# A graph network on one core: the round loop written out, and the leaky ReLU made by ScalarE's Prelu

## The reference

```python
h = jnp.maximum(_layernorm(x, axis=-1), 0.0)
x = x + _L0_gnn_ref(h, adj, ...)      # attention, then two hops
h = jnp.maximum(_layernorm(x, axis=-1), 0.0)
x = x + _L1_gnn_ref(h, adj, ...)      # three graph convolutions
# in L0:
Xw = X @ Wv + bv
e = jax.nn.leaky_relu(sj[:, None, :] + si[:, :, None] + ab[0], negative_slope=0.2)
alpha_matrix = A * jnp.exp(e)
transition = alpha_matrix / (jnp.sum(alpha_matrix, axis=-1, keepdims=True) + 1e-12)
for k in range(3):
    H = H + Xk @ Wk[k] + bk[k]
    Xk = jnp.einsum('bij,bjd->bid', transition, Xk)
return jax.nn.relu(H)
```

## Time and profile before

| what | value |
|---|---|
| median of 3 runs | 897.61 us (896.24 to 898.79) |
| the profiled execution | 896.19 us |
| its span (first to last instruction) | 894.2 us |
| instructions in the trace | 22245 |
| TensorE matmul busy | 873.0 us |
| VectorE busy | 780.2 us |
| ScalarE busy | 629.5 us |
| GpSimd busy | 443.3 us |
| granted TensorE clock, mean | 0.994 of full speed |

### The profile page before, as it was taken

How to read it: one execution, slowest core, us unless ns; L and a number is a source line. 1 busy time by engine, 2 the same in 40 slices (tenths; PEclk the granted TensorE clock), 3 DMA queues, 4 the chain that set the end, 5 groups by cost and what they waited for, 6 DMA issues and landing times.

```text
span 894.2 us, 22245 instructions
## 1 busy us (share of the span) xinstructions
PE 873.0 (98%) x6480; PEld 818.2 (92%) x6480; DVE 780.2 (87%) x2065; ACT 629.5 (70%) x1543; POOL 443.3 (50%) x532
## 2 busy tenths in 40 slices
PE   8799999999999999999999999999999999999996
PEld 7699999899998999989999999998999999999996
DVE  5789999899898999989999899989999899999972
ACT  4477777677777777777777677776777677777773
POOL 4455454455454455455454455454555454555552
PEclk9899999999999999999999999999999999999999
DMA  8112122122121122121121121121121121221001
GB/s 195 41 32 56 35 60 59 32 59 54 34 59 48 41 59 55 34 59 46 43 59 50 39 59 46 43 59 41 48 59 45 44 59 41 48 59 47 26 26 35
DMA packets 107819, 45.44 MB, mean 51 GB/s; under 512 B 72560, under 2 KB 107504, under 8 KB 107760
## 3 DMA queue, kind: packets, MB, share of 16 engines
q1 hardware_dynamic: 106672, 43.81, 19.4%
q10 hardware_dynamic: 1088, 1.05, 0.4%
HBM read 28.05 MB, written 16.78 MB: 50 GB/s over the span
## 4 chain that ended last, share of the span: by engine, by line
PE 92%; issue 2%; DVE 1%; SPq 1%; POOL 1%; ACT 1%; DMA 1%; DVEq 0%; ACTq 0%; POOLq 0%
PE bank L873 41%; PE bank_p L873 35%; PE bank_turned L873 6%; PE bank_T L873 4%; PE bank_turned L884 3%; PE bank_T L894 2%; SPq L272 1%; DMA bias_col<-in_L_gnn_b 1%; ACT s_hi L517 0%; DVE h0T_lo L639 0%; POOL w_gcn_lo L372 0%; DVE p0b L716 0%; PE bank_p L1029 0%; POOL y__lo L345 0%; POOL bias_h L388 0%
## 5 line engine op out<-in xcount | busy, mean ns | idle before, releaser
L345 POOL TENSOR_TENSOR y__lo<-y_full,y__hi 128x256 fp32r<-128x256 f32 x256 | 191.5, 762 | 101.0 <-ACT y_full L534 101.0
L336 POOL TENSOR_TENSOR rstd<-veps,minus_half 128x2 f32<-128x2 f32 x128 | 95.5, 746 | 250.6 <-DVE veps L606 250.6
L873 PE MATMUL bank_p<-w_p_hi,h0T_hi 128*128 128x258 f32 (+1 forms) x512 | 176.4, 360 | 1.0 <-POOL w_p_lo L367 1.0
L873 PE MATMUL bank_p<-w_p_lo,h0T_hi 128*128 128x258 f32 (+1 forms) x512 | 165.3, 339 | 0.0
L873 PE MATMUL bank_p<-w_p_hi,h0T_lo 128*128 128x258 f32 (+1 forms) x512 | 142.7, 340 | 5.9 <-DVE h0T_lo L639 5.9
L873 PE MATMUL bank<-w_gcn_hi,y__hi 128*128 128x256 f32 x512 | 132.9, 292 | 1.5 <-ACT y__hi L534 1.3
L873 PE MATMUL bank<-w_gcn_lo,y__hi 128*128 128x256 f32 x512 | 127.9, 283 | 0.0
L534 ACT ACTIVATE y__hi<-bank,bias_col 128x256 fp32r<-128x256 f32 x256 | 119.8, 468 | 3.0 <-PE bank L873 3.0
L534 ACT ACTIVATE y_full<-bank,bias_col 128x256 f32<-128x256 f32 x256 | 121.7, 475 | 0.0
L361 POOL TENSOR_TENSOR adjT_lo<-adjT_full,adjT_hi 128x256 fp32r<-128x256 f32 x64 | 64.5, 1008 | 85.5 <-ACT adjT_hi L440 85.5
L873 PEld LDWEIGHTS bank_p<-w_p_hi,h0T_hi 128*128 128x128 f32 x512 | 97.3, 190 | 7.2 <-POOL w_p_lo L367 1.2
(11 more groups left out here) (94 smaller groups left out, 2346.7 us busy)
## 6 DMA issues: line engine op xcount, KB each, us to landing
x_in<-in_x SPq DMA_DIRECT2D x64, 256.0 KB, 2.9
x_new<-x_out SPq DMA_DIRECT2D x64, 256.0 KB, 2.2
adj_blocks<-in_adj SPq DMA_DIRECT2D x256, 32.0 KB, 2.1
w_raw<-in_L_gnn_Wk ACTq DMA_DIRECT2D x3, 256.0 KB, 6.9
w_raw<-in_L_gnn_W SPq DMA_DIRECT2D x3, 256.0 KB, 5.8
bk_bc<-in_L_gnn_bk SPq DMA_DIRECT2D x1, 384.0 KB, 6.2
wv_raw<-in_L_gnn_Wv ACTq DMA_DIRECT2D x1, 256.0 KB, 3.7
aw_bc<-in_L_gnn_aw SPq DMA_DIRECT2D x1, 256.0 KB, 5.4
```

The lines of the kernel that those rows point to most:

```text
L336: pool.tensor_tensor(rstd[n][k % 2][:], veps[n][k % 2][:], minus_half[:], ALU.pow)\
L345: pool.tensor_tensor(y[n][1][:, c], y_full[n][:, c], plain(y[n][0][:, c]), ALU.subtract)\
L873: return pe.matmul(dst, stationary, moving, start=start, stop=stop, skip_group_check=True)
```

## The change

The loop goes: `rounds(one)` calls `one(i, i % ROUND)` for i from 0 to 66, so each engine's program is straight-line code, with plain numbers in every wait. ScalarE's `logits` uses Prelu with alpha = 0.2 where it used Identity, so `z` holds the leaky ReLU at once. VectorE's instruction and the semaphore `leaky_made` go, and `exponentials` waits for `z_made`, which ScalarE itself raises.

```diff
-        def rounds(eng, one):
-
-
-            for i in range(ROUND):
-                one(i, i)
-            with eng.Fori(0, N_PAIRS // BODY - 1) as turn:
-                for k in range(BODY):
-                    one(turn * BODY + (ROUND + k), k % ROUND)
-            for i in range(N_PAIRS - ROUND, N_PAIRS + LAG_D):
+        def rounds(one):
+
+            for i in range(N_PAIRS + LAG_D):
                 one(i, i % ROUND)
...
         def after(i, n):
 
-            return not isinstance(i, int) or i >= n
+            return i >= n
...
-                act.activation(z[k % 2][:, 0, :], spread_ps[:, 0, :], ACT.Identity, bias=uv[k % 2][:, 0, 0:1])
-                act.activation(z[k % 2][:, 1, :], spread_ps[:, 1, :], ACT.Identity, bias=uv[k % 2][:, 1, 0:1])\
-                   .then_inc(z_made, 1)
+                for g in range(G):
+                    last = act.activation(z[k % 2][:, g, :], spread_ps[:, g, :], ACT.Prelu,
+                                          bias=uv[k % 2][:, g, 0:1], alpha=SLOPE)
+                last.then_inc(z_made, 1)
 
             def exponentials(i, k):
-                act.wait_ge(leaky_made, i + 1)
+                act.wait_ge(z_made, i + 1)
...
-            def leaky(i, k):
-                dve.wait_ge(z_made, i + 1)
-                zz = z[k % 2][:]
-                dve.scalar_tensor_tensor(zz, zz, SLOPE, zz, ALU.mult, ALU.max).then_inc(leaky_made, 1)
...
                 if a is not None:
-                    leaky(a, k)
                     turn_adj(a, k)
```

More of the change, by code:

```diff
@@ L40 @@
 ROUND = 4
-BODY = 2 * ROUND
 LAG_B, LAG_C, LAG_D = 1, 2, 3
@@ L193, in gnn_kernel @@
         z_made = sem("z_made")
-        leaky_made = sem("leaky_made")
         exp_made = sem("exp_made")
@@ L215, in gnn_kernel @@
         out_made = sem("out_made")
-        def rounds(eng, one):
-            for i in range(ROUND):
-                one(i, i)
-            with eng.Fori(0, N_PAIRS // BODY - 1) as turn:
-                for k in range(BODY):
-                    one(turn * BODY + (ROUND + k), k % ROUND)
-            for i in range(N_PAIRS - ROUND, N_PAIRS + LAG_D):
+        def rounds(one):
+            for i in range(N_PAIRS + LAG_D):
                 one(i, i % ROUND)
         def here(i, lag):
-            if isinstance(i, int) and not 0 <= i - lag < N_PAIRS:
-                return None
-            return i - lag
+            return i - lag if 0 <= i - lag < N_PAIRS else None
         def first(i):
-            return isinstance(i, int) and i == 0
+            return i == 0
         def second(i):
-            return isinstance(i, int) and i == 1
+            return i == 1
         def tail(i):
-            return isinstance(i, int) and i >= N_PAIRS
+            return i >= N_PAIRS
         def after(i, n):
-            return not isinstance(i, int) or i >= n
+            return i >= n
         def landed(i, k):
@@ L312, in one @@
                     store(n, (k - LAG_D) % ROUND)
-            rounds(sp, one)
+            rounds(one)
             for k in range(ROUND):
@@ L408, in one @@
                     gcn_weights_low()
-            rounds(pool, one)
+            rounds(one)
         @block.scalar
@@ L573, in one @@
                     adjT_high(a, k)
-            rounds(act, one)
+            rounds(one)
         @block.vector
@@ L800, in first_round @@
                 p2_low(0, 0)
-                leaky(0, 0)
                 moments(0, 1, 1, lambda: attention(0, 0))
@@ L861, in one @@
                     p0_bias(a, k)
-            rounds(dve, one)
+            rounds(one)
         @block.tensor
@@ L1072, in one @@
                     z1_product(b)
-            rounds(pe, one)
+            rounds(one)
 _OUT = "x_new"
```

## The result

The changed kernel takes 882.42 us (median of 4 runs, 881.72 to 883.34) against 897.22 us before (median of 4 runs). The ratio is 0.9834, with a 95% interval of 0.9817 to 0.9851: 1.7% faster, where 1.1% was forecast.

The account below looks back on a forecast made before the run. TensorE, busy 873.0 of 894.2 us, was taken as the bound. The 56 rounds -11.2, pauses +2.0, start and end -0.5 made -9.7 us, so 887.9 us on the median's scale; range 885.5 to 893.9.

Parts of the forecast that it names:

- the mechanisms of the back edges and of `rstd`: Loop branches stall VectorE's sequencer; GpSimd's `rstd` is held 0.12 us by the leaky ReLU's two SBUF operands.
- The wait at `aT_hi`: TensorE's weight load in each round: earlier `rstd` closes the wait, rounds of 13.23 us, 56 rounds -11.2 us with edges.
- The pauses: VectorE sequencer stops at code-block changes in straight-line code: about 7 in 56 rounds, +2.0 us.
- Start and end: Rounds 0 to 3 gain 0.2 us and rounds 60 to 63 gain 0.3 through the same chain: -0.5 us.
- The edges: Six loop back edges, VectorE waiting before `h0T_lo`, 1.2 us each: -7.1 us once written out.
- the 9.0 us lost: Loop's 56 rounds take 752.11 us against 743.1 at ordinary length; split into 1.9 for pauses and 7.1 for edges.
- Prelu in place of Identity: ScalarE's two activations from PSUM: same time as Identity's 368 and 360 ns; rival of slow Prelu, chance 0.02.
- VectorE's 0.42 us as such: Leaky ReLU's busy time in each of 64 rounds, mostly off TensorE's path: its removal by itself gains nothing.
- One table load: ScalarE: Prelu shares Exp's table; rival of separate tables, 2.57 us of loads a round, about 980 us, chance 0.05.
- The other bound of `rstd`: Rival on GpSimd: the transpose holds `rstd` at 0.81 us too, rounds of 13.31, 893.3 us, chance 0.26.
- The stream as the bound: Rival: instruction fetching of straight-line code stops engines; 909 us at two in three stops, up to 921, chance 0.05.
- No pause at all, 885.5: Low end of the forecast range: written-out code in which no block change falls on TensorE's path.

Follow-up runs that it names:

- the run with a short body: Kernel before with 4 rounds in the loop's body instead of 8, so 13 back edges instead of 6: 888.14 us, ratio 0.9902.
- the shifted loop: Loop kept, leaky ReLU left out, VectorE's code moved by 8 idle single-column writes at its start: 888.46 us, ratio 0.9908 to before.
- with `hb` in PSUM: `hb` written back to its PSUM bank: on the changed kernel 876.68 us (0.9779); written out with leaky ReLU on VectorE 876.86 us (0.9783).

## Why the prediction was wrong, step by step

The direction held, and so did the mechanisms of the back edges and of `rstd`. The sizes of three terms did not, all to the same side, and together they are the 4.6 us between 9.7 and 14.3.

- *The wait at `aT_hi`, mis-sized: -11.2 us for the 56 rounds was forecast, -13.3 without pauses was measured.* The failing step is "TensorE waits 0.04 in loop code and 0.07 in straight-line code, so both waits close". That figure came from one step of the earlier trace rows. A weight load that is late delays the first matmul and stretches the distance to the second as well; the wait was 0.15 in the loop (0.50 for both steps against 0.35 with nothing waited for) and 0.18 in written-out code (0.53), and did not close but fell to 0.07. TensorE followed `aT_hi` ns for ns: the round went from 13.31 to 13.19 when `rstd` went from 0.81 to 0.70. A cap of 0.08 was set where 0.18 was there to be had.
- *The pauses: +2.0 us forecast, about +0.15 measured* (a round of 13.30 and one of 13.23). The step "one pause of 0.3 for 14 blocks makes 7 in 56 rounds" took the loop's rate for the straight-line code's. In the loop the block edge falls on the same instruction in each turn, so that one unlucky place is counted seven times. In straight-line code it walks through the round. With the leaky ReLU on VectorE it met an exposed place seven times, just as many as forecast; with one instruction fewer in each round it met one, before `adjT_full` in round 34 (13.20 us, no cost). How many are exposed is luck of placement: 4 idle writes took all seven away. The 0.11 of the round of 13.30, round 23, is GpSimd's, and the "issue" before `alpha` stands in that round too. `y_lo` begins 0.30 late there and is then held by `x` (its two instructions take 1.89 us instead of 1.44, as the rows of the section on the result show). All eight written-out kernels have `y_lo` late by 0.30 in this same round, however VectorE's code was moved, so it belongs to a place in GpSimd's code. What stops it there was not tried. It lengthens the round only where ordinary ones are 13.19.
- *Start and end: -0.5 forecast, -1.1 measured*, of which 0.63 is in round 0 (11.52 against 12.15), where kernels differ anyhow, and 0.45 behind round 60, the same wait as above where 0.3 was forecast.
- *The edges: -7.1 us, nearly right.* Six of 1.2 are in the trace of before; the run with a short body shows that they go without writing anything out. The split of the 9.0 us lost was slightly off: the 0.08 of the round of 13.35 was put down to the pause at `alpha`, but that round also stands before each edge of the short body and of the shifted loop, where nothing pauses at `alpha`. So it is the edge's, 1.27 in all, and a pause cost 0.20 to 0.23. The total stays the same.
- *Costed at nothing, rightly:* Prelu in place of Identity (364 ns against 368 and 360), the second wait on `z_made`, VectorE's 0.42 us as such. One table load.
- *The other bound of `rstd`*, that the transpose holds it, falls: it ran beside the transpose at 0.70.
- *The stream as the bound* falls too. The instruction queues moved 53 blocks of 16 KB and 56 packets of mostly 8 KB, against 13 and 46 before, and none of the 56 rounds is more than 0.11 us longer than the ordinary one.

The range was too narrow at its low end. "No pause at all, 885.5" was taken as the best case while the chain's gain was treated as certain to 0.01 us a round; 56 rounds turn an error of 0.04 into 2.2 us. (Its ends are also a little off by the prediction's own sums, without weight for the outcome: no pause at all is 887.9 - 2.0 = 885.9, and 893.3 with one pause more is 893.6.)

## What to carry to other kernels

When a TensorE wait recurs in every round, measure it over all matmuls from the last undisturbed one to the next undisturbed one, not at the first that is late; small waits multiply by the number of rounds. A VectorE instruction can cost time through what it reads: ask of each one with two SBUF operands which GpSimd instruction runs beside it, and whether one operand could stay in PSUM. Before a hardware loop is written out, try a body short enough to be kept, and look for "issue" behind the branch; an instruction added or removed ahead of a loop that does not fit can change its price.

## What the runs showed that was not expected

- Taking one instruction out of a loop's body made an edge cost 3.0 us instead of 1.2, and eight idle instructions ahead of the loop took that back (56 rounds: 756.61 and 745.11 us).
- Where a change of block in VectorE's code is seen at all, VectorE stops for 0.29 to 0.31 us (0.44 before `alpha` with `hb` in PSUM). It was seen before `alpha`, `x_out` and `adjT_full` only, at 7 of some 24 places; moving the code by 4 instructions took all seven away.
- Round 0 took from 11.5 us (the change) to 14.4 (the loop without the leaky ReLU) in kernels that do the same there, and the granted TensorE clock in it was 1.00 in some and 0.87 to 0.88 in others, among them all those above 12.9. What sets this was not tried; it makes spans of single profiles differ by 2 us.
